# A pipelined audio block: the last tile's turn moved away from the batch's border, two pieces of its work put into the next batch

## The reference

```python
q = (x @ Wq).reshape(b, n, 8, 64) * 64 ** -0.5
sim = einsum('pbnhd,pkhd->pbnhk', (x @ Wq_pk) split in 2 halves, pk_keys)   # 64 keys a half
scores, idx = top_k(sim, 16)                    # for each of 2 halves, 8 heads
score = scores[0][..., :, None] + scores[1][..., None, :]   # 16 x 16 pairs
final_scores, final_indices = top_k(score, 16), the row numbers idx0 + 64 * idx1
w = softmax(final_scores)
k = sum(w * keys_table[final_indices]);  v = sum(w * values_table[final_indices])
attn = softmax(causal(q @ k.T));  out = (attn @ v) @ Wo
```

## Time and profile before

| what | value |
|---|---|
| median of 3 runs | 5366.33 us (5365.53 to 5366.68) |
| profiled execution | 5371.56 us |
| its span in the profile | 5369.7 us |
| PE, DVE, ACT, POOL busy | 81%, 77%, 42%, 49% |
| instructions | 104279 |
| granted TensorE clock, mean | 0.94 of full |

### The profile page before, as it was taken

One profiled execution on the slowest core, in us unless ns is written; L12 is line 12 of the kernel. 1 busy time (PEld: TensorE's weight loads), 2 busy tenths in 40 slices (PEclk: granted clock), 3 DMA queues, 4 the chain that ended last, 5 costly groups with the idle time before them and its releaser, 6 DMA issues.

```text
span 5369.7 us, 104279 instructions
## 1 busy us (share of the span) xinstructions
PE 4336.4 (81%) x28033; PEld 2830.8 (53%) x28033; DVE 4139.9 (77%) x16757; ACT 2279.4 (42%) x5575; POOL 2657.5 (49%) x2915
## 2 busy tenths in 40 slices
PE   5677775057889888888888888888888888888888
PEld 4555552024555555555555555555555555555556
DVE  4677776668888878887878888888888888878843
ACT  4333333023444444444444444444444444444444
POOL 0011111343566656566656656656656665656661
PEclk8999997578999999999999999999999999999998
DMA  1000002012323232323232323233332323232321
GB/s 45 1 0 0 0 0 54 24 48 61 100 78 104 78 100 77 102 79 101 77 99 78 101 77 105 86 92 89 94 91 86 97 84 99 81 101 77 104 77 53
DMA packets 160561, 389.31 MB, mean 73 GB/s; under 512 B 65847, under 2 KB 69943, under 8 KB 159612
## 3 DMA queue, kind: packets, MB, share of 16 engines
q1 hardware_dynamic: 78876, 215.14, 12.7%
q0 software_dynamic: 81120, 167.81, 12.0%
HBM read 379.87 MB, written 4.61 MB: 72 GB/s over the span
## 4 chain that ended last, share of the span: by engine, by line
DVE 28%; PE 23%; issue 17%; another core or an unknown queue 10%; ACT 4%; DVEq 1%; DMA 0%; ACTq 0%; POOL 0%; POOLq 0%
PE ps L1043 22%; DVE w L1763 6%; DVE topi L1585 4%; DVE miss L1705 2%; ACT ex L1391 2%; DVE top L1579 2%; DVE sc L1591 2%; DVE miss L1710 1%; DVE cs L1591 1%; DVE sm L1773 1%; DVE fin L1579 1%; PE ps L1238 1%; DVE left L1515 1%; DVE wmat L1559 1%
## 5 line engine op out<-in xcount | busy, mean ns | idle before, releaser
L1030 POOL DMA_INDIRECT rows<-table_dram,idxT x2528 | 2569.2, 1016 | 1783.8 <-issue 663.9
L1043 PE MATMUL ps<-w,dtab 128*128 128x375 f32 (+1 forms) x6144 | 1784.3, 424 | 15.4 <-issue 13.8
L1763 DVE SCALAR_TENSOR_TENSOR w<-ps,ex 128x750 f32<-128x750 f32 (+1 forms) x1152 | 1107.6, 961 | 526.5 <-remote 170.1
L1043 PEld LDWEIGHTS ps<-w,dtab 128*128 128x128 f32 x6144 | 1033.4, 198 | 401.7 <-issue 77.6
L1391 ACT ACTIVATE ex<-ps 128x750 f32<-128x750 f32 (+1 forms) x1152 | 947.6, 823 | 607.9 <-PE ps L1043 368.0
L1043 PE MATMUL ps<-rank_dense,half 128*128 128x375 bf16 (+1 forms) x2432 | 557.6, 320 | 223.8 <-DVE w L1763 177.8
L1043 PE MATMUL ps<-parts,half 128*128 128x375 bf16 x2176 | 547.7, 333 | 78.5 <-ACT ex L1391 50.2
L1043 PEld LDWEIGHTS ps<-rank_dense,half 128*128 128x128 bf16 x2432 | 209.0, 99 | 679.7 <-DVE w L1763 381.4
L491 POOL COPY states<-n_h 64x32 f32 (+1 forms) x375 | 76.8, 205 | 748.4 <-DVE n_h L480 748.4
L382 PE MATMUL ps<-which,bias 128*64 128x256 bf16 (+2 forms) x3123 | 397.5, 280 | 8.7 <-DVE which L461 8.7
L1585 DVE FIND_INDEX8 topi<-top,sc 125x8 uint32<-125x64 f32 x1536 | 306.5, 220 | 40.1 <-issue 38.7
(11 more groups left out here) (227 smaller groups left out, 6312.5 us busy)
## 6 DMA issues: line engine op xcount, KB each, us to landing
dtab<-dense_dram SPq DMA_DIRECT2D x256, 512.0 KB
dtab<-corner_dram SPq DMA_DIRECT2D x128, 512.0 KB
rows<-table_dram,idxT POOLq DMA_INDIRECT x2528
xin<-x_dram SPq DMA_DIRECT2D x16, 187.5 KB
early<-early_dram SPq DMA_DIRECT2D x1, 1800.5 KB, 9.0
half<-halves_dram POOLq DMA_DIRECT2D x1, 1680.0 KB, 12.8
rows_in<-hh SPq DMA_DIRECT2D x16, 93.8 KB, 2.2
rows_in<-uu SPq DMA_DIRECT2D x16, 93.8 KB, 2.2
```

What stands on the lines that cost most here:

```text
L1030: nc.gpsimd.indirect_dma_start(out=rows[:, PLACES[u] * GROUP + j, :], out_offset=None, in_=table[:, :], in_offset=bass.IndirectOffsetOnAxi ...
L1043: return nc.tensor.matmul(out_, lhsT, rhs, start=start, stop=stop, skip_group_check=open_bank)
L1763: nc.vector.scalar_tensor_tensor(w[:, p % 2, :, 0:wide], ps[:, 2:4, 0:wide], float(K), ex[:, p % 2, :, 0:wide], ALU.is_lt, ALU.mult).then_ ...
```

## The change

The last tile's slices get fewer. cand_rows goes to LATE, so for this tile it is done in the next batch, just before away_0. The slice weights is split for all tiles into weights (the sum) and shares (reciprocal and ewd), and for the last tile shares goes to LATE too, before index. With less to do before it, the last tile's rank and turn fall on steps 68 and 69 in place of 69 and 70. The turned copies of the first two tiles, which stood between the slices of the two tiles in their step, now stand behind all slices of the step. The table of PE's loads is written anew, the step length goes from 3.32 to 3.35, and the window of part 0 from steps 56 to 62 to steps 63 to 65; with these several small products change their step (the sum of unit 3 from 15 to 17 and of unit 9 from 58 to 56, value 3 from 35 to 32 and value 6 from 59 to 61, query 6 from 25 to 48, query 2 from 56 to 59, query 0 from 57 to 62, the first turn from 31 to 33). The links are waits of DVE on its own earlier results; the last tile has one more.

```diff
--- before.py
+++ after.py
@@ -643,7 +643,7 @@
     *by_groups("next", 2 * H, 0.128), *by_groups("nwhere", 2 * H, 0.2), ("lists", 0.9), ("cand", 0.95), ("cand_rows", 0.85),
     *by_groups("best", H, 0.12), ("bwhere", 0.8), *by_groups("bstrike", H, 0.18), *by_groups("bnext", H, 0.12), ("blast", 1.55),
     ("exponents", 0.8), ("counts", 1.8), ("miss_0", 1.25), ("fold_0", 1.2), ("miss_1", 1.25), ("fold_1", 1.2),
-    ("miss_2", 1.25), ("weights", 1.0), ("fold_2", 1.2), ("miss_3", 1.25), ("fold_3", 1.2), ("miss_4", 1.25), ("fold_4", 1.2),
+    ("miss_2", 1.25), ("weights", 0.3), ("shares", 0.6), ("fold_2", 1.2), ("miss_3", 1.25), ("fold_3", 1.2), ("miss_4", 1.25), ("fold_4", 1.2),
     ("miss_5", 1.25), ("fold_5", 1.2), ("found", 1.6),
     ("away_0", 1.85), ("near_0", 1.8), ("away_1", 1.85), ("near_1", 1.8),
     ("ready", 0.5), ("sums", 0.2),
@@ -651,7 +651,7 @@
 LATE = [
     ("miss_3", 1.25), ("fold_3", 1.2), ("miss_4", 1.25), ("fold_4", 1.2), ("miss_5", 1.25), ("fold_5", 1.2), ("found_b", 0.9),
     ("miss_0", 1.25), ("fold_0", 1.2), ("miss_1", 1.25), ("fold_1", 1.2), ("found_c", 0.6),
-    ("away_0", 1.85), ("near_0", 1.8), ("index", 0.4),
+    ("cand_rows", 0.45), ("away_0", 1.85), ("near_0", 1.8), ("shares", 0.35), ("index", 0.4),
 ]
 
 
@@ -663,7 +663,7 @@
 
 ITEMS = [(h, c) for h in (7, 0, 1, 2, 3, 4, 5, 6) for c in range(NT)]
 OLD = 5 * NT
-STEP = 3.32
+STEP = 3.35
 SIM_AT = [2 + m * 8 // 3 for m in range(len(ITEMS))]
 TURN_AT = [at + 4 for at in SIM_AT]
 QUERY_IN = {4: (6, 36), 6: (10, 52), 0: (26, STEPS - 3), 2: (44, STEPS - 3)}
@@ -673,14 +673,18 @@
 AHEAD = 4
 SCORE_AT = 3
 LATE_TURN_AT = 9
-PART_IN = {1: (3, 9), 2: (17, 24), 3: (33, 40), 4: (42, 54), 0: (56, 62)}
+PART_IN = {1: (3, 9), 2: (17, 24), 3: (33, 40), 4: (42, 54), 0: (63, 65)}
 
 
 def places():
 
     dve, act, bank = {}, {}, ({}, {})
     vector = [1.2 if p >= CORNER else 0.9 for p in range(STEPS + 8)]
-    tensor = [2.6 if p >= CORNER else 3.2 if p % HALF == 0 else 2.25 if p % 8 == 0 else 1.95 for p in range(STEPS + 8)]
+    tensor = [1.95 + (0.6 if p > CORNER or p == 0 else 0.0) for p in range(STEPS + 8)]
+    for h in range(DH):
+        tensor[(h * HALF - 1) % STEPS] += 1.3
+        tensor[h * HALF + HALF // 2 - 1] += 0.33
+    tensor[CORNER - 1] += 0.95
 
     def slot(which, earliest, key, cost):
         at = earliest
@@ -1504,7 +1508,7 @@
             dve.wait_ge(s_code, 16)
             nc.vector.nop().then_inc(s_fd, 1)
 
-            LINKS = [38, 38, 44]
+            LINKS = [38, 38, 45]
             links = [0]
 
             def part_left(i, n):
@@ -1532,7 +1536,8 @@
                     for name, _ in slices(c):
                         if dve_at[name, c] == p:
                             front_slice(name, c, kind, b)
-                    if c < LASTC and dve_at["turned", c] == p:
+                for c in range(LASTC):
+                    if dve_at["turned", c] == p:
                         dve.wait_ge(s_um, b * LASTC + (c + 1))
                         if not is_first(f0 + c, NT):
                             dve.wait_ge(s_rf, b * NU + (EATEN[c] - NU + RING))
@@ -1652,7 +1657,9 @@
                                                         cst["secondkey"][0:TT].unsqueeze(1).broadcast_to([TT, gh, K]),
                                                         ALU.mult, ALU.add))
                 if name == "cand":
-                    add_lists(top, cs, H, top[:, 0:H], top[:, H:2 * H])
+                    last = add_lists(top, cs, H, top[:, 0:H], top[:, H:2 * H])
+                    if c == LASTC:
+                        link(last)
                 if name == "cand_rows":
                     linked()
                     link(add_lists(topf, ci[:, 0:gh], gh, topf[:, 0, 0:gh], topf[:, 1, 0:gh]))
@@ -1725,6 +1732,7 @@
                 if name == "weights":
                     dve.wait_ge(s_fexp, f + 1)
                     nc.vector.tensor_reduce(esum[:], ew[:], AX_X, ALU.add).then_inc(s_es, 1)
+                if name == "shares":
                     dve.wait_ge(s_es, f + 1)
                     link(nc.vector.reciprocal(einv[:, 0:gh], esum[:, 0:gh]))
                     linked()
@@ -1737,6 +1745,7 @@
                         linked()
                     elif c == LASTC:
                         dve.wait_ge(s_eq2, b * 2 + 2)
+                        linked()
                     else:
                         dve.wait_ge(s_eq, f + 1)
                     link(nc.vector.tensor_tensor(away[:], posx[:, h:h + 2, :].unsqueeze(3).broadcast_to([TT, 2, K, CAND]),
```

## The result

| | before | after |
|---|---|---|
| median of 5 runs each | 5366.68 us (5365.53 to 5379.22) | 5407.93 us (5383.72 to 5413.14) |
| ratio, 95% interval | | 1.006 [1.004, 1.0079] |
| profiled execution | 5371.56 us | 5383.72 us |

The forecast was 5351 us, range 5322 to 5384. The profiled execution of the changed kernel was the fastest of its five, so its trace carries only 12 of the 41 us. They lie in the loop (3681.7 to 3689.8 us, +8.1) and behind it (the last batch and the end, 286.2 to 291.7, +5.5); the part ahead of the loop got 1.5 shorter. The record has the mean granted clock of the executions without a trace too: 0.929, 0.932, 0.930 and 0.931, against 0.934 in the profiled one.

A forecast was written before the change was run, and what follows sets the result against it. Neither PE (81% busy) nor DVE (77%) was a plain bound; 42 us of DVE idle time a batch was at stake. Terms -7 - 8.5 - 5 + 5 + 0 = -15.5 us, less 5.2 for the median, gave 5351 us, range 5322 to 5384.

The forecast's parts named there:

- the one on the moves: Small products and sums changing step: net 0, plus or minus 0.8 us a batch, 12 us in all.
- The border: Batch border: last tile's turn one step earlier lets the next batch's first exponent start sooner, 0.45 us x 15, -7 us.
- the hold -8.5: About 3.1 us standstill at PE's wait for the last turn, 9 of 15 borders; middle of 0 and 17 us.
- the windows under 20.5 us: Sign at the border: from w of step 67 to the next batch's w, under 20.5 us on average.
- the exponent right behind the last ranks: Sign at the border: next batch's first exponent directly follows the last ranks, without the 3.61 us of idle time.
- the copy more than 2 us ahead of it: Sign at the border: ACT's u_front copy for the last tile over 2 us ahead of the first exponent.
- both forms have a second hold at the loop's return: Long and short borders both hold again at the loop's return; PE idle 2.23 us in the short example.
- about a third be absorbed: At the loop's return: a copy 3.1 us later lengthens the border only 1.9 us, so 0.65 of a gain passes on.
- Step 56: Second tile's turned copies: four index searches ahead hide DVE's wait, 0.36 us a batch, -5 us in all.
- Step 34: First tile's turned copies free bank 6 later for the gathered sum; w of step 36 0.2 to 0.3 late, +5 us.
- the "over 1 us": Sign of error: steps 33 to 37 taking over 1 us more than before.
- the slower rival: First tile's copies at step 34's end hold bank 6 against the gathered sum, 1.8 us a batch: 5386 us, chance 0.19.

The follow-up runs named there:

- e16: The changed kernel unaltered, run again on another chip: 5387.41 us, 1.0032 of the kernel before there.
- e5: The changed kernel unaltered, run again on another chip: 5463.89 us, 0.9998 of the kernel before there.
- e7: Kernel before with 128 semaphore increments ahead of PE's attention program, shifting its code in memory: 5467.06 us, 0.9994 of before.
- e2: Kernel before with only the turned copies moved behind all slices of their step: 5475.16 us, 1.0007 of before.
- e3: Kernel before with only the new table of PE's loads, step length 3.35 and window of part 0: 5479.92 us, 1.0009 of before.
- e4: Changed kernel without the new place of the turned copies: 5462.16 us, 0.9982 of before.
- e8: Changed kernel with 128 semaphore increments ahead of PE's attention program, shifting its code in memory: 5462.65 us, 0.9987 of before.
- e1: Kernel before with only the late lists (cand_rows and shares into the next batch, weights split): 5504.99 us, 1.0063 of before.
- e10: Changed kernel with 31 idle products a batch in nine places where PE waits: 5424.96 us, 0.9908 of before.
- e6: Changed kernel without the turned copies' move, repeated on another chip: 5462.34 us, 0.9985 of before.
- e15: Changed kernel with 38 idle products a batch in PE's waits, seven more than e10: 5355.15 us, 0.9974 of before.
- e11: Kernel before with idle products at the border only, four ahead of step 71's wait and four at batch end: 5476.90 us, 1.0008 of before.

## Why the prediction was wrong

**The step that failed** is the one on the moves: "Net 0, but each such move shifts where PE's own holds fall: plus or minus 0.8 us a batch, 12 us in all". I took their cost for a scatter without a direction. The new order has other waits of PE, and behind them the clock falls more often: 273.1 and 344.7 us in two executions of the changed kernel (the first, and e16) against 228.7. At 0.45 us each that is 20 us for the first profile. The other four executions of the first comparison were on average 26 us slower still. Their traces were not taken, but by their mean clocks they had some 40 to 45 us more at the lower clock, which at 0.45 is 18 to 20 of the 26; and e16's loop is 34.2 us longer than the first, with 71.6 us more at the lower clock, 0.48 each. What the runs do not show is that each of the moves makes such a wait: the link from the new order to the lower clock is read from these sums. Nor is all of it the clock: in steps 38 to 47 the new order costs some 1.4 us a batch beside it, as shown below. And it depends on the chip, for e5 has no more time at the lower clock than the kernel before beside it, and no loss.

Less the 20 us, the first profile's loop would be 12 us shorter than before, not far from the -15.5 forecast. On the slower chips this reckoning gives no such gain (e7 and e5: 3606.5 and 3610.4 us), and the parts below do not stand where the forecast has them, so I don't claim it.

**The border (-7, and the hold -8.5: 1.03 us a batch).** From w of step 67 to w of step 1: 24.20 to 23.20 us, a gain of 1.00, and 0.84 in e16. The sum was right by luck and the reason for the larger half was not: the hold went in some of the batches only (4 of 14 still have it, where 8 had), and step 0 behind the border gives back 1.78 of the 2.78 us. Of the signs, the windows under 20.5 us and the exponent right behind the last ranks came true; the copy more than 2 us ahead of it did in 2 of 14 batches, in the others it is 1.66 to 1.95.

What took the hold's place is PE's pause at the loop's return, between the front ranks and the next product of parts. In the kernel before, w of step 71 is held (3.4 to 4.7 us idle ahead of it) in 9 of 14 batches, and the pause behind it is 0.2 us or less in 8 of them and 1.4 in one, the one in the earlier trace rows; in the 5 batches without the hold it is 1.5 to 2.2 us. So the prediction's "both forms have a second hold at the loop's return" holds for one held batch only. In the changed kernel the pause is 2.0 to 5.6 us in 13 of 14 batches, also where the hold is gone; the mean rises from 0.8 to 3.2 us. e2 and e7 have the old picture (over 1 us in 4 of 14), e3, e4, e5, e8 and e16 the new one (13 of 14). Taking away the wait for the turn mostly uncovers the wait at the return: of 2.78 us gained ahead of it 1.78 do not pass on, where the prediction lets about a third be absorbed.

**Step 56 (-5: 0.36 a batch).** What the text prices happened: idxT's idle time fell from 18.2 to 7.1 us (the line is for the whole execution; in the loop it is 6.9). Copies group, changed kernel:

```profile
L1560 DVE CAST idxT<-ps 64x63 uint32<-64x63 f32 (+1 forms) x128 | 25.6, 200 | 7.1 <-issue 4.6 <-ACT ex L1395 1.4
```

But steps 55 to 58 went from 15.93 to 17.06 us. The sum of unit 9, which I had noted as moved from step 58 to 56 and priced at nothing, now stands there, and PE waits for w right ahead of it. Timeline, changed kernel:

```profile
2129.53 0.26 ACT L1357 COPY u_front<-ps 6x125 f32<-6x125 f32 x1 [3.70 <-remote]
2130.89 0.46 DVE L1560 CAST idxT<-ps 64x63 uint32<-64x63 f32 x2
2131.00 0.49 PE L1047 MATMUL ps<-rank_dense,half 128*128 128x375 bf16 x2 [2.52 <-DVE w L1772]
```

Yet I can't lay it on that move: e3 and e4 have 17.23 and 17.25 us there, and e1, where the sum is still in step 58, 17.31; the old order and e2 have 16.08 (e7) and 16.65 on such chips. Every other order of the small products brought a us here, and the runs don't show by what. The clock alone is not it: e7 has 3.3 us a batch at the lower clock in these steps, the changed kernel 3.2.

**Step 34 (+5: 0.33 a batch).** Steps 33 to 37: 19.46 to 20.18, so 0.72, twice the estimate, and short of the "over 1 us" that I had set as the sign of an error. The idle PE ahead of the sum is there, 1.6 to 2.0 us in all 14 batches:

```profile
2052.36 1.37 DVE L1564 TENSOR_TENSOR wmat<-ps,cst 64x504 f32<-64x504 f32 x2
2053.86 1.93 PE L1047 MATMUL ps<-rows,wmat 128*32 128x128 f32 x32 [1.97 <-DVE wmat L1564]
```

The w of step 36 comes 7.66 us behind that of step 34, where the text reckons 6.9; in e10, with no lower clock in these steps, it is 7.12. e4 and e6 with the old copies have 19.85 and 19.89 for steps 33 to 37. So the mechanism of the slower rival is real in the trace and decides nothing: before the change PE stood 1.6 to 3.1 us at the ranks of this step, a wait that it now has less of (2.1 to 2.2 us in 4 of 14, under 0.9 in the others).

**Work over the border (0).** Steps 6 and 7 grew by 0.90 us, as the text has it; steps 59 to 66 gave back 1.51 in the first profile and 0.47 in e16. The bound of 7.5 us covers it.

**Where nothing was counted.** Steps 38 to 47 grew by 2.03 us a batch (33.41 to 35.44), the dearest piece of all. Here the lower clock is at work too: of its stretches 13 begin in steps 37 to 43 of the changed kernel and 7 in the one before. But it is the smaller part: 3.11 us a batch at the lower clock against 1.78 are worth 0.6 us, and e7, the old order with 3.23, takes 33.87. What else the trace shows is where places puts DVE's slices. DVE has 0.75 us more work in these steps (30.36 to 31.11), and its load is uneven: step 42 has 1.46 us in place of 2.90, step 44 has 3.78 in place of 2.69. In step 42 DVE then stands idle for 2.64 us ahead of the next w, waiting for ACT's ex, where it stood 0.65. With e10's fillers, and no lower clock in these steps, that wait is 1.50 and the steps take 34.57; with those of e15 they take 34.30. The prediction counts nothing for slices that change their step, beyond the ones it names.

**The rule of the Trainium skill** (Runtime: NRT & Kernel Launch, Instruction fetch mechanics) on the taken branch: the pause is there, 5.55 us in the rows of the border above, with a code packet near it, and in the last batch of the loop, where the branch is not taken, neither kernel has one. What the prediction drew from it, that a wait taken out ahead of the branch moves the fetch forward and so passes on in full, is not borne out: the first exponent comes 2.2 us earlier after w of step 67, and step 0 behind the return grows from 3.21 to 4.99 us.

## What to carry to other kernels

Read the clock's column of a window beside its length: where the clock is low, ask what PE did just before, for in the stretches shown here it had stood idle, and the price comes later, where PE sets the pace. A change of order must be priced by the waits of PE that it makes, not only by the work that it moves. Products without meaning in PE's waits can more than pay for themselves (0.6% against the changed kernel, 0.3 to 0.9% against the kernel before), and only there: the same ones where PE is busy cost 1.5%. A change of half a per cent has to be measured on more than one chip.

## What was new about the hardware

- Executions of one program differ in their time at the lower clock: the changed kernel's loop had 273.1 and 344.7 us on two like chips and 320.8 on a slower one. That goes far to explain its wide runs: of the twelve in e16 the three under 5380 us have a mean clock of 0.932 to 0.936, the four over 5400 us one of 0.928 to 0.931.
- Between chips the same kernel differs by 2% (5366 to 5477 us). The part ahead of the loop takes nearly the same time on both kinds, 1401.9 us and 1410.8 (e7), and DVE in the loop is as busy (3091.7 and 3097.1). More time at the lower clock (228.7 and 303.8 us, at 0.45 some 34 us) is about half of the loop's 62 us. The rest is open.
- The late releases of 3 us at the border come in about two of three batches of the kernel before; batches 3, 6, 9 and 12 are free of them on every chip with a trace of the old border (before, e2, e7, e11), with the code shifted too. What sets them is open; neither the clock (e11) nor the code's place (e7) does.
- Four products of zeros (eight records) took 1.98 us in the wait of e15, and POOL, ACT and DVE did not get slower: over the loop they are busy for 2259, 1698 and 3092 us, in the changed kernel for 2250, 1699 and 3092.
